# A DLRM tower's interaction layers: three low parts by the adding DMA, 14 tiles split, and the remainder taken from the gathered rows

## The chip, the cores and the metric

One core of one Trainium2 chip. The metric is the device time of one execution in microseconds (us); lower is better. The engines are TensorE (PE in the profile), VectorE (DVE), ScalarE (ACT), GpSimd (POOL) and SyncE (SP), which here only issues DMAs.

## The reference, cut to what matters

For each of B = 1024 samples, 32 ids are looked up in 32 tables of 64-wide rows. Two interaction layers follow, each with a ReLU, whose results are summed over the 64 columns; a small dense network ends it.

```
e = stack([tbl_f[ids[:, f]] for f in range(32)], axis=1)          # (1024, 32, 64)
cin(h, h0, W, b) = relu(einsum('bhd,bmd,ohm->bod', h, h0, W) + b)
x1 = cin(e, e, W1, b1)                                            # 128 outputs
x2 = cin(x1[:, :64], e, W2, b2)                                   # 128 outputs
z  = concat([x1[:, 64:], x2], axis=1).sum(-1)
h  = relu(concat([z, dense_ctx], 1) @ W_top1 + b_top1)
h  = relu(h @ W_top2 + b_top2);  y = h @ W_top3
```

## The kernel before, in words

The samples go in 128 chunks of 8; a chunk has N = 8 x 64 = 512 columns. Two chunks are a pair. Every engine runs a loop of 128 steps (`all_steps`), written by hand, one step for each chunk c; the order of the work is that of the lines in each engine's `step`, and semaphores join the engines. Each engine carries out its own list strictly in order, so what stands behind a wait waits too.

**Gathering.** GpSimd gathers the rows of a pair with four indirect DMAs (L271) into `gathered[s]` (128 partitions, partition = table x 4 + a quarter of the pair's samples), after a small copy of the indices (`place_idx`, L266). SP stores them twice to `emb_rows` in HBM (`store_rows`, L354), so that feature f + shift can be read for any f.

**Layer 1** uses the symmetry of the products: the pairs of features are ordered by their distance (shift). Four tiles `near` (shifts 0 to 15, L239) times `h0` (L236) are multiplied by GpSimd into `prod1` (L308), and go through TensorE as four full-precision tiles of 2 matmuls each (`tiles1`, L592). The products of distance 16 are the *remainder*: 16 for a sample, made from `rem_a` and `rem_b` (`load_rem`, L348, two loads of SP from `emb_rows` for a pair), multiplied by GpSimd (L279), cast to a high part twice by ScalarE (L727, L728), with a low part by GpSimd (L295), all in `rem_parts` of 96 partitions, which one matmul a chunk reads (L595). ScalarE adds the bias, takes the ReLU and the sums (L713, `layer1`, 8 activations of 64 columns).

**Layer 2.** SP copies the first 64 rows of `x1` to all partitions (`replicate_x1`, L248, two DMAs), ScalarE copies them to PSUM (`copy_x1rep`, L762), and VectorE multiplies them with `near` into `pnear` (8 tiles) and with `far` into `pfar` (8 tiles), both L514. Of the 16 tiles 13 are *split* (`T_SPLIT`): a high part in `phi`, rounded by ScalarE (L789 for near tiles 2 to 7, L790 for tiles 0 and 1, L801 for 5 far tiles), and a low part `plo` = product - high part, made by VectorE (L519) for tiles 2 to 12. For the first `T_DMA` = 2 tiles the low part is made otherwise: ScalarE writes the negated high part (L788, `minus_ready`) and an adding DMA of GpSimd adds the product (`low_parts`, L285). A split tile costs 3 matmuls (L604, L605, L610), the other 3 tiles (`whole`, L615) cost 2 slow ones each.

**The steps.** In step c, TensorE does the near high parts of chunk c, layer 1 of chunk c + 2, then `whole`, `low` and the far high parts of chunk c. ScalarE does `layer1(c + 1)`, the minus part, the near casts, the copy of `x1rep` for c + 1, the far cast (behind `acc2_ready` of the chunk before) and `layer2(c - 1)`. SP waits for `z1_ready` of c + 2 (that is `layer1(c + 1)`), replicates `x1`, loads `near` of chunk c + 3 (five DMAs, when VectorE has made `pnear` of c), in even steps stores gathered rows, then loads `far` of c + 2, and in even steps last the remainder rows. In step c of before, TensorE's layer 1 waits for `p1_ready` (L308) and `rem_lo_ready` (L295).

Of the kernel before, what the change touches and what calls it, by code (L numbers as in the profile page):

```python
# [6 lines left out]
F = 32  # L7
D = 64
# [27 lines left out]
T_DMA = 2  # L36
T_FAR = T_NEAR + K2
T_SPLIT = T_FAR + 1
# [4 lines left out]
def build_dlrm(nc, a):  # L43
# [7 lines left out]
    with ctx:  # L51
# [15 lines left out]
        idx = [sb(f"idx_{s}", [P, PAIR_GATHERS], i32) for s in range(3)]  # L67
# [63 lines left out]
        idx_ready = sem("idx_ready")  # L131
# [20 lines left out]
        x1p_ready = sem("x1p_ready")  # L152
        rem_in = sem("rem_in")
# [102 lines left out]
        def _(pool):  # L256
# [8 lines left out]
            def place_idx(pair, s):  # L265
                nc.gpsimd.tensor_copy(idx[s][:, :].unsqueeze(2), idx_all[:, :, bass.ds(pair, 1)]).then_inc(idx_ready, 1)  # L266
                pool.wait_ge(idx_ready, pair + 1)
                pool.sem_inc(lookups_begun, 1)

            def gather(g, s):  # L270
                nc.gpsimd.indirect_dma_start(  # L271
                    out=gathered[s][:, g, :], out_offset=None, in_=a["tables"],
                    in_offset=bass.IndirectOffsetOnAxis(ap=idx[s][:, g:g + 1], axis=0)).then_inc(rows_gathered[s], 16)

            def remainder_products(pair):
                pool.wait_ge(rem_in, 32 * pair + 32)

                pool.wait_ge(rem_lo_ready, pair)
                nc.gpsimd.tensor_tensor(rem_prod[:, :], rem_a[:, :], rem_b[:, :], ALU.mult).then_inc(rem_prod_ready, 1)  # L279
# [8 lines left out]
            for pair in range(3):  # L288
                place_idx(pair, pair)
                for g in range(PAIR_GATHERS):  # L290
                    gather(g, pair)

            def remainder_low(pair):
                pool.wait_ge(rem_hi_ready, pair + 1)
                nc.gpsimd.tensor_tensor(rem_parts[2 * REM:3 * REM, :], rem_prod[:, :],  # L295
                                        rem_parts[0:REM, :].bitcast(fp32), ALU.subtract).then_inc(rem_lo_ready, 1)

            def step(c, turn, u, at):
                pair, odd = turn * (U // 2) + u // 2, u % 2
                if at == 0:  # L300
                    pool.wait_ge(rem_prod_ready, 2)
                    remainder_low(1)
                    pool.wait_ge(rem_lo_ready, 2)
# [8 lines left out]
                if odd and within(at, 3):  # L312
                    remainder_products(pair + 2)
                if not odd and begun(at) and within(at, 2):

                    pool.wait_ge(p1_ready, c + 3)
                    remainder_low(pair + 1)
                    pool.wait_ge(rem_lo_ready, pair + 2)
                if within(at, 7 - odd):
                    if not odd:  # L320
# [4 lines left out]
                        place_idx(pair + 3, u // 2)  # L325
                    for g in range(2 * odd, 2 * odd + 2):
                        gather(g, u // 2)

            remainder_products(1)
# [3 lines left out]
        def _(sp):  # L333
# [28 lines left out]
            store_copy(sp, 0, 0, 0)  # L362
            sp.wait_ge(emb_stored, STORES)
            load_h0(sp, 0, 0, 0)
            load_near_tiles(sp, 0, 0, range(0, K1 // 2))
            load_rem(0)
            load_near(sp, N, 1, 1)
            store_rows(1, 1, 1)
            load_far(0, 0)
            sp.wait_ge(emb_stored, 2 * STORES)  # L370
            sp.wait_ge(rem_prod_ready, 1)
            load_rem(2 * N)
            sp.wait_ge(z1_ready, 1)
            replicate_x1(sp, [0])

# [18 lines left out]
            def step(c, turn, u, at):  # L394
# [33 lines left out]
        def _(dve):  # L428
# [10 lines left out]
            dve.wait_ge(idx_ready, 2)  # L439
# [48 lines left out]
            def products1(s, ks):  # L488
# [7 lines left out]
            dve.wait_ge(rem_in, 32)  # L496
            nc.vector.tensor_tensor(rem_prod[:, :], rem_a[:, :], rem_b[:, :], ALU.mult).then_inc(rem_prod_ready, 1)
# [4 lines left out]
            dve.wait_ge(rem_hi_ready, 1)  # L502
            nc.vector.tensor_tensor(rem_parts[2 * REM:3 * REM, :], rem_prod[:, :],
                                    rem_parts[0:REM, :].bitcast(fp32), ALU.subtract).then_inc(rem_lo_ready, 1)
# [16 lines left out]
            def step(c, turn, u, at):  # L521
# [28 lines left out]
        def _(pe):  # L550
# [43 lines left out]
            def remainder1(s):  # L594
# [245 lines left out]
```

## Time and profile before

| what | us |
|---|---|
| median of 3 runs | 2034.03 |
| lowest and highest of them | 2031.25, 2035.14 |
| the profiled execution | 2035.26 |
| its span in the trace | 2033.5 |
| TensorE busy | 1999.9 |
| VectorE busy | 1923.5 |
| ScalarE busy | 1713.6 |
| GpSimd busy | 1647.3 |
| granted TensorE clock, mean | 0.997 |

The profile is of one execution. "Busy" is the union of the times in which an engine had an instruction under way; the rest is waiting. The span runs from the first to the last instruction of the program; the execution's own time is 1.8 us more.

### The profile page before, as it was taken

Reading aid. Unit: us, or ns where it says so; the run is one execution under the profiler, and the core shown is the slowest. Engines: PE = TensorE matmul, PEld = TensorE weight load, DVE = VectorE, ACT = ScalarE, POOL = GpSimd, SP = SyncE. Lnnn points to the kernel's source line nnn. Section 1 sums busy time; section 2 is a strip of 40 time slices with the busy share of each in tenths; the row PEclk is TensorE's granted clock in tenths of the full one; section 3 lists DMA queues with packets and bytes.
Section 4 is the critical chain, followed back from the end, with each engine's and each line's share of the span. In section 5 each row is a group of like instructions: output and inputs, shape, how many; then the busy total and the mean of one; then the engine's idle time right before and its main releaser. Section 6 shows DMA issues by size and latency. Waiting matters only on the chain.

```text
span 2033.5 us, 24093 instructions
## 1 busy us (share of the span) xinstructions
PE 1999.9 (98%) x7038; PEld 1325.8 (65%) x7038; DVE 1923.5 (95%) x546; ACT 1713.6 (84%) x4887; POOL 1647.3 (81%) x708
## 2 busy tenths in 40 slices
PE   5999999999999999999999999999999999999999
PEld 3666666666666666666666666666666666666664
DVE  6999999999999999999999999999999999999991
ACT  4788888888888888888888888888888888888873
POOL 5898887879899998887889998788999988887520
PEclk9999999999999999999999999999999999999999
DMA  7898988988988989989989989989988989989950
GB/s 227 217 268 235 245 246 232 245 248 232 245 249 234 248 244 235 250 241 236 253 237 237 254 237 236 257 232 237 257 233 238 255 231 239 255 230 238 251 131 11
DMA packets 257782, 474.16 MB, mean 233 GB/s; under 512 B 35425, under 2 KB 52321, under 8 KB 257522
## 3 DMA queue, kind: packets, MB, share of 16 engines
q1 hardware_dynamic: 230450, 396.18, 64.5%
q0 software_dynamic: 26624, 75.52, 22.0%
q8 instruction: 56, 0.92, 0.2%
q10 hardware_dynamic: 576, 0.92, 0.1%
q14 instruction: 76, 0.62, 0.1%
HBM read 321.49 MB, written 16.78 MB: 166 GB/s over the span
## 4 chain that ended last, share of the span: by engine, by line
PE 90%; DMA 3%; DVE 2%; ACT 2%; issue 2%; POOL 1%; SPq 0%; DVEq 0%; POOLq 0%; ACTq 0%
PE acc L592 20%; PE acc L604 17%; PE acc L605 17%; PE acc L610 17%; PE acc L615 14%; DMA plo<-pnear 2%; DVE pnear L514 2%; PE acc L595 1%; ACT phi L789 1%; ACT x L713 1%; POOL prod L308 1%; DMA x1rep<-x 1%; PE x1p L686 0%; DMA near<-emb_rows 0%; PE acc L686 0%
## 5 line engine op out<-in xcount | busy, mean ns | idle before, releaser
L271 POOL DMA_INDIRECT gathered<-in_tables,idx x256 | 655.4, 2560 | 101.8 <-POOL idx L266 51.2
L308 POOL TENSOR_TENSOR prod<-near,h 128x2048 f32<-128x2048 f32 x126 | 582.5, 4623 | 128.5 <-PE acc L595 81.1
L604 PE MATMUL acc<-phi,w2lo 128*128 128x512 f32 x1664 | 655.2, 394 | 8.2 <-ACT phi L789 8.0
L605 PE MATMUL acc<-phi,w2hi 128*128 128x512 f32 x1664 | 654.3, 393 | 0.0
L514 DVE TENSOR_TENSOR pnear<-near,x1p 128x4096 f32<-128x4096 f32 x128 | 564.9, 4413 | 6.2 <-ACT x1p L762 3.8
L514 DVE TENSOR_TENSOR pfar<-far,x1p 128x4096 f32<-128x4096 f32 x128 | 564.9, 4413 | 0.7 <-PE acc L615 0.7
L592 PE MATMUL acc<-prod,w1T 128*128 128x512 f32 x1024 | 460.1, 592 | 1.5 <-DVE prod L489 1.5
L610 PE MATMUL acc<-plo,w2hi 128*128 128x512 f32 x1664 | 454.5, 423 | 0.0
L713 ACT ACTIVATE x<-acc,bias 128x64 f32<-128x64 f32 x1024 | 305.8, 324 | 170.6 <-PE acc L595 170.6
L519 DVE TENSOR_TENSOR plo<-pnear,phi 128x3072 fp32r<-128x3072 f32 x128 | 446.2, 3486 | 0.3 <-ACT phi L789 0.3
L519 DVE TENSOR_TENSOR plo<-pfar,phi 128x2560 fp32r<-128x2560 f32 x128 | 361.2, 2822 | 45.1 <-ACT phi L801 45.0
L610 PEld LDWEIGHTS acc<-plo,w2hi 128*128 128x128 f32 x1664 | 313.0, 188 | 120.6 <-issue 61.0
L604 PEld LDWEIGHTS acc<-phi,w2lo 128*128 128x128 f32 x1664 | 314.1, 189 | 82.3 <-ACT phi L789 12.8
L605 PEld LDWEIGHTS acc<-phi,w2hi 128*128 128x128 f32 x1664 | 314.1, 189 | 67.9
L789 ACT CAST phi<-pnear 128x3072 fp32r<-128x3072 f32 x128 | 352.7, 2756 | 0.0
L615 PE MATMUL acc<-pfar,w2T 128*128 128x512 f32 x768 | 350.6, 592 | 0.0
L592 PEld LDWEIGHTS acc<-prod,w1T 128*128 128x128 f32 x1024 | 193.6, 189 | 197.0 <-issue 184.5
L801 ACT CAST phi<-pfar 128x2560 fp32r<-128x2560 f32 x128 | 299.5, 2340 | 0.0
L713 ACT ACTIVATE acc<-acc,bias 128x64 f32<-128x64 f32 x1024 | 293.5, 291 | 4.8 <-PE acc L605 4.8
L615 PEld LDWEIGHTS acc<-pfar,w2T 128*128 128x128 f32 x768 | 145.7, 190 | 159.3 <-issue 153.7
L713 ACT ACTIVATION_READ_ACCUMULATOR x<-acc,bias 128x1 f32 x1024 | 220.9, 216 | 0.0
L713 ACT ACTIVATION_READ_ACCUMULATOR acc<-acc,bias 128x1 f32 x1024 | 218.1, 213 | 0.0
(75 smaller groups left out, 1151.3 us busy)
## 6 DMA issues: line engine op xcount, KB each, us to landing
far<-emb_rows SPq DMA_DIRECT2D x512, 256.0 KB, 4.6
near<-emb_rows SPq DMA_DIRECT2D x510, 256.0 KB
plo<-pnear POOLq DMA_DIRECT2D x128, 512.0 KB
x1rep<-x SPq DMA_DIRECT2D x255, 256.0 KB, 4.3
h<-emb_rows SPq DMA_DIRECT2D x128, 256.0 KB
emb_rows<-gathered SPq DMA_DIRECT2D x127, 128.0 KB
gathered<-in_tables,idx POOLq DMA_INDIRECT x256, 6.6
rem_a<-emb_rows SPq DMA_DIRECT2D x64, 64.0 KB
```

The costliest lines, as they stand in the source:

```text
L271: nc.gpsimd.indirect_dma_start(out=gathered[s][:, g, :], out_offset=None, in_=a["tables"], in_offset=bass.IndirectOffsetOnAxis(ap=idx[s][: ...
L308: nc.gpsimd.tensor_tensor(prod1[:, :, :], near[(u + 2) % 3][:, :, :], h0[odd][:, :].unsqueeze(1).to_broadcast([P, K1, N]), ALU.mult).then_ ...
L514: return nc.vector.tensor_tensor(out, h0part.unsqueeze(1).to_broadcast([P, A2, k, N]), x1p[s][:, :].rearrange("p (a n) -> p a n", a=A2).un ...
L519: return nc.vector.tensor_tensor(plo[:, parts, :], whole, phi[:, parts, :].bitcast(fp32), ALU.subtract)
L592: nc.tensor.matmul(acc1[s][:, :], w1T[:, k, :], prod1[:, k, :], start=(k == 0), stop=False)
L604: nc.tensor.matmul(acc2[s][:, :], w2lo[:, t, :], phi[:, t, :], start=(t == T_DMA), stop=False)
L605: mm = nc.tensor.matmul(acc2[s][:, :], w2hi[:, t, :], phi[:, t, :], start=False, stop=(t == T_SPLIT - 1))
L610: mm = nc.tensor.matmul(acc2[s][:, :], w2hi[:, t, :], plo[:, t, :], start=False, stop=False)
L615: mm = nc.tensor.matmul(acc2[s][:, :], w2T[:, k, :], pfar[:, 1, K2 - T_WHOLE + k, :], start=False, stop=False)
L713: ins = nc.scalar.activation(out[:, cols], acc[:, cols], ACT.Relu, bias=bias[:, :], accum_out=z[:, bass.ds(c * CB + b, 1)])
L789: nc.scalar.copy(phi[:, T_DMA:T_NEAR, :], products[:, T_DMA:T_NEAR, :]).then_inc(hi_near_ready, 1)
L801: nc.scalar.copy(phi[:, T_NEAR:T_SPLIT, :], pfar[:, :, :, :].rearrange("p a k n -> p (a k) n")[:, 0:T_SPLIT - T_NEAR, :]).then_inc(hi_far_ ...
```

## The change

`T_DMA` goes from 2 to 3 and `T_SPLIT` from 13 to 14, so that 2 tiles stay whole. The gathers read their indices from `idx_all` itself, without the copy. The remainder no longer comes from `emb_rows`: its lower features stand in partitions 0 to 63 of `gathered`, its upper ones are moved beside them by one DMA (`move_upper`); product, high part and low part are made in that layout (64 partitions, 256 elements), and three DMAs a pair (`place_remainder`) carry them to their places in `rem_parts`, of which there are two now. TensorE waits for these DMAs (`rem_in`). ScalarE casts the far tiles ahead of the copy of `x1rep`, and the three tiles of the adding DMA after that; TensorE takes these tiles' high parts behind layer 1. The wait of SP for the stores is at the near load of odd steps.

```diff
-T_DMA = 2
+T_DMA = 3
-T_SPLIT = T_FAR + 1
+T_SPLIT = T_FAR + 2
...
+        rem_b = sb("rem_b", [HALF * GS, PAIR_GATHERS, D])
+        rem_prod = sb("rem_prod", [HALF * GS, PAIR_GATHERS * D])
+        rem_hi = sb("rem_hi", [HALF * GS, PAIR_GATHERS * D], fp32r)
+        rem_lo = sb("rem_lo", [HALF * GS, PAIR_GATHERS * D], fp32r)
+        rem_parts = [sb(f"rem_parts_{s}", [3 * REM, N], fp32r) for s in range(2)]
...
@@ GpSimd
+            def gather(g, pair, s):
...
+                    in_offset=bass.IndirectOffsetOnAxis(ap=idx_all[:, g, pair:pair + 1], axis=0)).then_inc(rows_gathered[s], 16)
+            def remainder_products(pair, s):
+                pool.wait_ge(rem_b_in, 16 * pair + 16)
+                if pair:
+                    pool.wait_ge(rem_lo_ready, pair)
+                nc.gpsimd.tensor_tensor(rem_prod[:, :], gathered[s][0:HALF * GS, :, :].rearrange("p g d -> p (g d)"),
+                                        rem_b[:, :, :].rearrange("p g d -> p (g d)"), ALU.mult).then_inc(rem_prod_ready, 1)
+            def remainder_low(pair):
+                pool.wait_ge(rem_hi_ready, pair + 1)
+                nc.gpsimd.tensor_tensor(rem_lo[:, :], rem_prod[:, :], rem_hi[:, :].bitcast(fp32),
+                                        ALU.subtract).then_inc(rem_lo_ready, 1)
             def step(c, turn, u, at):
                 pair, odd = turn * (U // 2) + u // 2, u % 2
+                if not odd and begun(at) and within(at, 2):
+                    remainder_low(pair + 1)
                 if within(at, 2):
...
                 low_parts(c)
                 if odd and within(at, 3):
-                    remainder_products(pair + 2)
-                if not odd and begun(at) and within(at, 2):
-
-                    pool.wait_ge(p1_ready, c + 3)
-                    remainder_low(pair + 1)
-                    pool.wait_ge(rem_lo_ready, pair + 2)
+                    remainder_products(pair + 2, (u // 2 + 2) % 3)
...
@@ SP
+            def move_upper(pair, s):
+                if pair:
+                    sp.wait_ge(rem_prod_ready, pair)
+                sp.dma_start(rem_b[:, :, :], gathered[s][HALF * GS:F * GS, :, :]).then_inc(rem_b_in, 16)
+            def place_remainder(pair):
+                sp.wait_ge(rem_lo_ready, pair + 1)
+                if pair >= 2:
+                    sp.wait_ge(acc1_ready, 2 * pair - 2)
+                for b, part in enumerate((rem_hi, rem_hi, rem_lo)):
+                    home = rem_parts[pair % 2][b * REM:(b + 1) * REM, :].rearrange("r (w n) -> r w n", w=2)
+                    sp.dma_start(home.bitcast(fp32), part[:, :].bitcast(fp32)).then_inc(rem_in, 16)
...
                     sp.wait_ge(pnear_ready, c + 1)
                     sp.wait_ge(p1_ready, c + 2)
+                    if odd:
+                        sp.wait_ge(emb_stored, STORES * (pair + 3))
                     load_near(sp, (c + 3) * N, 1 - odd, u % 3)
+                if not odd and begun(at) and within(at, 2):
+                    place_remainder(pair + 1)
                 if not odd and within(at, 5):
                     store_rows(pair + 2, (u // 2 + 2) % 3, turn + (u // 2 + 2) // 3 + 1)
+                    move_upper(pair + 2, (u // 2 + 2) % 3)
                 if within(at, 2):
                     sp.wait_ge(pfar_ready, c + 1)
                     load_far((c + 2) * N, odd)
-                if not odd and within(at, 5):
-                    sp.wait_ge(emb_stored, STORES * pair + 3 * STORES)
-                    sp.sem_inc(stores_begun, 1)
-                    sp.wait_ge(rem_prod_ready, pair + 2)
-                    load_rem((c + 4) * N)
@@ VectorE, step
                     dve.wait_ge(lo_near_ready, c)
+                    dve.wait_ge(hi_dma_ready, c)
@@ TensorE, step
                 high(odd, range(T_DMA, T_NEAR))
-                pe.wait_ge(hi_dma_ready, c + 1)
-                high(odd, range(0, T_DMA)).then_inc(hi_near_used, 1)
                 if within(at, 2):
                     pe.wait_ge(p1_ready, c + 3)
-                    pe.wait_ge(rem_lo_ready, pair + 2)
+                    pe.wait_ge(rem_in, 48 * (pair + 2))
                     pe.wait_ge(z1_ready, c + 1)
-                    layer1(odd)
+                    layer1(odd, pair + 1)
...
+                pe.wait_ge(hi_dma_ready, c + 1)
+                high(odd, range(0, T_DMA)).then_inc(hi_near_used, 1)
                 pe.wait_ge(pfar_ready, c + 1)
                 whole(odd).then_inc(far_used, 1)
@@ ScalarE, step
-                if not odd and within(at, 2):
-                    remainder_hi(pair + 1)
...
                 nc.scalar.copy(phi[:, T_DMA:T_NEAR, :], products[:, T_DMA:T_NEAR, :]).then_inc(hi_near_ready, 1)
-                nc.scalar.copy(phi[:, 0:T_DMA, :], products[:, 0:T_DMA, :]).then_inc(hi_dma_ready, 1)
+                act.wait_ge(pfar_ready, c + 1)
+                if begun(at):
+                    act.wait_ge(acc2_ready, c)
+                nc.scalar.copy(phi[:, T_NEAR:T_SPLIT, :], ...).then_inc(hi_far_ready, 1)
                 if within(at, 1):
...
                     copy_x1rep(1 - odd)
-                act.wait_ge(pfar_ready, c + 1)
-                if begun(at):
-                    act.wait_ge(acc2_ready, c)
-                nc.scalar.copy(phi[:, T_NEAR:T_SPLIT, :], ...).then_inc(hi_far_ready, 1)
+                nc.scalar.copy(phi[:, 0:T_DMA, :], products[:, 0:T_DMA, :]).then_inc(hi_dma_ready, 1)
+                if odd and within(at, 3):
+                    remainder_hi(pair + 2)
```

## Rows read from the trace of the kernel before

**Rows 1.** The page: busy us of each engine; the software queue's packets, MB, share.

```profile
PE 1999.9 (98%) x7038; PEld 1325.8 (65%) x7038; DVE 1923.5 (95%) x546; ACT 1713.6 (84%) x4887; POOL 1647.3 (81%) x708
...
q0 software_dynamic: 26624, 75.52, 22.0%
```

**Rows 2.** Chain of waits, 1000 to 1034 us: start us, us, what.

```profile
1001.68 2.58 PE acc L615 x6
1004.26 2.99 PE acc L610 x13
1007.24 0.23 PE acc L604
...
1013.20 3.43 PE acc L592 x8
1016.63 0.24 PE acc L595
...
1028.38 3.43 PE acc L592 x8
```

**Rows 3.** Groups by line and shape: busy us, mean ns of one | idle before.

```profile
L519 DVE TENSOR_TENSOR plo<-pnear,phi 128x3072 fp32r<-128x3072 f32 x128 | 446.2, 3486 | 0.3 <-ACT phi L789 0.3
L519 DVE TENSOR_TENSOR plo<-pfar,phi 128x2560 fp32r<-128x2560 f32 x128 | 361.2, 2822 | 45.1 <-ACT phi L801 45.0
L789 ACT CAST phi<-pnear 128x3072 fp32r<-128x3072 f32 x128 | 352.7, 2756 | 0.0
...
L801 ACT CAST phi<-pfar 128x2560 fp32r<-128x2560 f32 x128 | 299.5, 2340 | 0.0
L713 ACT ACTIVATE acc<-acc,bias 128x64 f32<-128x64 f32 x1024 | 293.5, 291 | 4.8 <-PE acc L605 4.8
...
L790 ACT CAST phi<-pnear 128x1024 fp32r<-128x1024 f32 x128 | 133.9, 1046 | 0.0
L762 ACT COPY x1p<-x1rep 128x1024 f32<-128x1024 f32 x128 | 129.3, 1010 | 11.4 <-DMA x1rep<-x 11.2
...
L728 ACT CAST rem_parts<-rem_prod 32x512 fp32r<-32x512 f32 x64 | 39.7, 620 | 0.8
```

**Rows 4.** Timeline, 1000 to 1034 us: start us, us, instruction [idle before <-releaser].

```profile
1006.97 4.61 SPq L242 DMA_DIRECT2D near<-emb_rows  x4
...
1015.88 4.41 DVE L514 TENSOR_TENSOR pnear<-near,x1p 128x4096 f32<-128x4096 f32 x1
...
1016.90 0.31 ACT L713 ACTIVATE x<-acc,bias 128x64 f32<-128x64 f32 x1 [1.47 <-PE acc L595]
...
1018.35 4.64 POOL L308 TENSOR_TENSOR prod<-near,h 128x2048 f32<-128x2048 f32 x1 [1.55 <-DMA near<-emb_rows]
...
1019.47 1.20 SPq L251 DMA_DIRECT2D x1rep<-x  x2
...
1022.00 4.45 SPq L242 DMA_DIRECT2D near<-emb_rows  x4
```

**Rows 5.** Timeline of the start, 28 to 57 us.

```profile
28.83 0.59 SPq L352 DMA_DIRECT2D rem_b<-emb_rows  x1
...
32.98 1.26 POOL L279 TENSOR_TENSOR rem_prod<-rem_a,rem_b 32x512 f32<-32x512 f32 x1 [6.17 <-DMA rem_b<-emb_rows]
...
48.16 0.99 POOL L285 DMA_DIRECT2D plo<-pnear  x1
...
56.49 4.42 DVE L514 TENSOR_TENSOR pnear<-near,x1p 128x4096 f32<-128x4096 f32 x1 [2.32 <-DMA plo<-pnear]
```

**Rows 6.** Stretches: busy of PE, PEld, DVE, ACT, POOL, then PEclk, DMA share, GB/s.

```profile
62.40:64.70 2.30, 0.01 (x1) 0.00 (x0) 2.30 (x1) 2.30 (x2) 2.10 (x2) 1.00 0.90 269
65.40:68.80 3.40, 3.40 (x10) 2.62 (x9) 3.11 (x1) 3.40 (x4) 3.10 (x2) 0.50 1.06 234
...
1980.20:1984.40 4.20, 0.09 (x1) 0.00 (x0) 4.20 (x2) 3.68 (x3) 0.85 (x1) 0.92 0.17 33
1984.50:1990.50 6.00, 6.00 (x14) 4.74 (x15) 6.00 (x3) 3.10 (x2) 0.00 (x0) 0.50 0.32 59
```

More of the change, by code:

```diff
@@ L288, in _ @@
             for pair in range(3):
-                place_idx(pair, pair)
                 for g in range(PAIR_GATHERS):
-                    gather(g, pair)
+                    gather(g, pair, pair)
+                pool.sem_inc(lookups_begun, 1)
             def remainder_low(pair):
                 pool.wait_ge(rem_hi_ready, pair + 1)
-                nc.gpsimd.tensor_tensor(rem_parts[2 * REM:3 * REM, :], rem_prod[:, :],
-                                        rem_parts[0:REM, :].bitcast(fp32), ALU.subtract).then_inc(rem_lo_ready, 1)
+                nc.gpsimd.tensor_tensor(rem_lo[:, :], rem_prod[:, :], rem_hi[:, :].bitcast(fp32),
+                                        ALU.subtract).then_inc(rem_lo_ready, 1)
             def step(c, turn, u, at):
                 pair, odd = turn * (U // 2) + u // 2, u % 2
[L300 to L303, printed above, removed]
+                if not odd and begun(at) and within(at, 2):
+                    remainder_low(pair + 1)
                 if within(at, 2):
@@ L324, in step @@
                         pool.wait_ge(emb_stored, STORES * pair + STORES)
-                        place_idx(pair + 3, u // 2)
+                        pool.wait_ge(rem_prod_ready, pair + 1)
                     for g in range(2 * odd, 2 * odd + 2):
-                        gather(g, u // 2)
-            remainder_products(1)
+                        gather(g, pair + 3, u // 2)
+            for pair in range(2):
+                remainder_products(pair, pair)
+                remainder_low(pair)
             all_steps(step)
@@ L362, in _ @@
             store_copy(sp, 0, 0, 0)
+            move_upper(0, 0)
             sp.wait_ge(emb_stored, STORES)
@@ L365, in _ @@
             load_near_tiles(sp, 0, 0, range(0, K1 // 2))
-            load_rem(0)
             load_near(sp, N, 1, 1)
             store_rows(1, 1, 1)
+            move_upper(1, 1)
+            place_remainder(0)
             load_far(0, 0)
             sp.wait_ge(emb_stored, 2 * STORES)
-            sp.wait_ge(rem_prod_ready, 1)
-            load_rem(2 * N)
             sp.wait_ge(z1_ready, 1)
             replicate_x1(sp, [0])
+            place_remainder(1)
             sp.wait_ge(tp_copied, 2)
@@ L592, in tiles1, with remainder1, layer1 @@
                     nc.tensor.matmul(acc1[s][:, :], w1T[:, k, :], prod1[:, k, :], start=(k == 0), stop=False)
-            def remainder1(s):
-                nc.tensor.matmul(acc1[s][:, :], w1remT[:, s, :], rem_parts[:, :],
+            def remainder1(s, pair):
+                nc.tensor.matmul(acc1[s][:, :], w1remT[:, s, :], rem_parts[pair % 2][:, :],
                                  start=False, stop=True).then_inc(acc1_ready, 1)
-            def layer1(s):
+            def layer1(s, pair):
                 tiles1(s, range(K1))
-                remainder1(s)
+                remainder1(s, pair)
             def high(s, parts):
@@ L622, in _ @@
             tiles1(0, range(K1 // 2, K1))
-            pe.wait_ge(rem_lo_ready, 1)
-            remainder1(0)
+            pe.wait_ge(rem_in, 48)
+            remainder1(0, 0)
             turn(6, *NEAR_TURNS[1])
@@ L627, in _ @@
             pe.wait_ge(p1_ready, 2)
-            layer1(1)
+            layer1(1, 0)
             pe.wait_ge(x1p_ready, 1)
@@ L726, in remainder_hi @@
                 act.wait_ge(rem_prod_ready, pair + 1)
-                nc.scalar.copy(rem_parts[0:REM, :], rem_prod[:, :])
-                nc.scalar.copy(rem_parts[REM:2 * REM, :], rem_prod[:, :]).then_inc(rem_hi_ready, 1)
+                if pair:
+                    act.wait_ge(rem_in, 48 * pair)
+                nc.scalar.copy(rem_hi[:, :], rem_prod[:, :]).then_inc(rem_hi_ready, 1)
             act.wait_ge(ident_ready, 1)
```

33 lines of the change are left out of this document (5 added, 28 removed).

## The prediction, made before the changed kernel was run

> **What bounds the kernel now.** I read the page first, then the chain of waits in one stretch of the middle, the groups by line and shape, the timeline of the same stretch, and last the start, where the queues are empty. The page [rows 1] shows TensorE busy for 1999.9 of 2033.5 us and VectorE for 1923.5. In the chain from 1000 to 1034 us [rows 2] there is nothing but matmuls end to end: 6 of `whole` in 2.58 us (0.43 each), 13 of `low` in 2.99 (0.23 each), one of `high` every 0.23, 8 of layer 1 in 3.43 and the remainder in 0.24. A chunk is 26 `high`, 13 `low`, 6 `whole`, 8 layer-1 and 1 remainder matmul: 39 x 0.23 + 14 x 0.43 + 0.24 = 15.2 us, and layer 1 starts at 1013.20 and again at 1028.38, 15.18 later. So TensorE sets the pace, 30.4 us for a pair of chunks. VectorE is next to it: 4.4 + 4.4 + 3.5 + 2.8 us = 15.1 [rows 3, 4]. The span is 2033.5 us, the profiled execution 2035.3, 1.3 above the median of 2034.0. About 0.2% (4 us) can be told from no change.
>
> **The change, part by part.**
> *14 tiles split.* `whole` loses 2 matmuls of 0.43, `high` and `low` gain 3 of 0.23: 0.69 - 0.86 = -0.17 us a chunk, x128 = -22 us [rows 2].
> *Three tiles by the adding DMA.* VectorE subtracts 5 near and 6 far tiles in place of 6 and 5, the same elements: 0. ScalarE: L788 and L790 go from 2 tiles to 3; by 1.05 us for 1024 elements and 2.34 for 2560 [rows 3] 1536 take 1.5, so +0.45 each; the near cast falls from 2.76 to 2.34, the far cast rises from 2.34 to 2.76. The software queue takes 22.0% of 16 engines, 447 us in all, 3.5 us a chunk [rows 1]; half as many bytes again bound the extra at 0 and 1.75 us of every DMA engine; I take 1.4, since gathers are a part of that queue.
> *Indices direct.* GpSimd loses 64 small copies and a wait in each. It is not on the path now: 0.
> *Remainder.* GpSimd's two operations shrink from 512 to 256 elements a partition, ScalarE has one cast of at most 0.62 us [rows 3] in place of two (I take 0.35, by half the elements). SP issues for a pair one load of `rem_b` and three placements instead of two loads; at 0.59 us an issue [rows 5] that is +1.2 us. **The place of it is what matters.** `place_remainder(pair + 1)` stands in SP's even step c *behind* `load_near(c + 3)`, and TensorE's `layer1` of the *same* step c now waits for it (`rem_in` of 48 x (pair + 2)). Before, only GpSimd's subtraction stood there.
> *`high(0..2)` behind layer 1.* Layer 1 is reached after 10 `high` matmuls, not 16: 1.4 us sooner. That helps GpSimd's product, and worsens any wait in front of layer 1.
> *Far cast ahead of the copy of `x1rep`.* It takes `acc2_ready` (the end of TensorE's chunk before) ahead of the copy, the dma cast, `layer2` and the next `layer1` on ScalarE, so all of them now start behind that end. Now VectorE waits only a little for the far cast; up to 0.35 us a chunk could be won, but TensorE would cover it.
>
> **When the placement lands.** Take the even step whose near product starts on VectorE at 1015.88 [rows 4]. SP starts to issue `x1rep` at R = 1019.47, and the four near loads from 1022.00 for 4.45 us, until R + 7.0. Three placements of 0.6 bring it to R + 8.8. The lower bound of landing: in the start, with few transfers under way, a remainder load ended its issue at 29.42 and GpSimd used it at 32.98, 3.6 later [rows 5]: R + 12.4. The upper: near loads whose issue ended at 1011.58 let GpSimd go at 1018.35, 6.8 later [rows 4]; the placements, in the same queue behind them, come at R + 7.0 + 6.8, plus up to 1.75 for the adding DMA, which is under way just then, plus 0.2: R + 15.7. I take R + 14.1, between them, nearer the crowded row. The same queue's order is on my side by the Trainium skill too (DMA: Bandwidth & Descriptors, section "Queues, rings and completion order"): on each DMA engine the descriptors are consumed in ring order. By the ~2 us fixed cost of that page (section "Anatomy of one DMA") alone it would be R + 10.8, an estimate, and 100 us less in the end.
>
> If nothing else moved, TensorE would want layer 1 at 4.4 (near product) + 1.5 (minus) + 2.3 (near cast) + 2.3 (10 `high`) behind 1015.88 = 1026.4, and get it at 1019.5 + 14.1 = 1033.6: **7 us idle in each even step**. It cannot be absorbed, since the loop closes. Call W the start of layer 1 in an even step.
> - W to the end of the chunk: layer 1 3.67, 6 `high` 1.37, 4 `whole` 1.72, 14 `low` 3.22, 12 `high` 2.75 = 12.7 [rows 2].
> - ScalarE from there, in its order: far cast 2.76, copy 1.01, dma cast 1.5, remainder cast 0.35, `layer2` 2.4 (8 x 0.29), `layer1` 2.4 (from 1016.90 to about 1019.4) = 10.4; with hand-offs 10.6 [rows 3, 4]. That is the next R. VectorE's branch is as long: far cast 2.76, subtraction of 6 tiles 3.5, near product 4.4 = 10.7.
> - R to the landing 14.1.
>
> Sum: 12.7 + 10.6 + 14.1 = 37.4 us for a pair against 30.4, TensorE idle for 37.4 - 30.0 = 7.4 of them.
>
> *The clock.* What TensorE does after such an idle time has rows: it stood still from 62.41 to 64.70, and the granted clock was 0.50 from 65.4 to 68.8; at the end it stood 4.2 us and ran at 0.50 from 1984.5 to 1990.5 [rows 6]. 3.4 and 6.0 us at 1.2 instead of 2.4 GHz lose 1.7 and 3.0; bounds 0 and 3.0. It falls on the W part of the loop, which is on the path. I take 2.1: 39.5 us a pair. The Trainium skill (TensorE: Matmul & The Clock Gate, section "HAM oscillation — how this bites in real kernels") tells of just this, a kernel that waits for a DMA in every tile and starts each one at half clock; without its effect here the forecast would be 2475.
>
> Even steps with the wait are c = 2 to 124, 62 of them: 62 x (39.5 - 30.4) = +564; start and end nearly as before: **2035 + 564 = about 2600, I say 2595 us**, 28% slower.
>
> **Rivals.**
> *A smaller stall.* Same mechanism, placements at R + 12.4 or sooner, no fall of the clock: 35.7 us a pair, 62 x 5.3 = +329, 2365 us; with near issues as quick as in an empty queue 2 us less again, 2240. For it: the longer period leaves DMA idle. Against: R is followed by near and adding transfers whatever the period. Chance 0.14.
> *TensorE stays the bound, faster.* The price would be the -22 us, 2013 us. It needs the placements to be landed by 1026.4, that is within R + 7.0, which is when the last near load has only been issued. For it: everything else fits, VectorE has no more work. It decides at a landing under R + 7.0; against it stand both rows of landing. Chance 0.09.
> *The adding DMA is the limit.* In the start it was issued at 48.16 and VectorE could go on at 56.49, 8.3 later [rows 5]. Half more bytes make it up to 10; minus ready at 5.9 + 10 = 15.9 against 15.1: at most 0.8 a chunk, +100 us, together with -22 some 2075-2110. It would need the remainder to be hidden. Chance 0.07.
> The forecast has the rest, 0.70.
>
> **Numbers.** Highest case: R + 15.7 and 3.0 of clock, 42.0 a pair, 62 x 11.6: 2755. The likeliest case alone spans 2400 to 2755. For 8 in 10 I go down into the first rival: 2260 to 2740. Faster 0.09 (second rival), within 0.2% 0.03 (out of the third), slower 0.88.
>
> **What would show it.** TensorE idle 6 to 8 us ahead of layer 1 (L592) in every second chunk, released by a DMA into `rem_parts`, 62 times, 400 us or more in all, and none in odd steps; TensorE's busy share near 80%; granted clock below 1 all through the middle; layer-1 starts alternating between about 17 and 22 us apart. On ScalarE the far cast starts right behind TensorE's last `high`. VectorE waits before the far subtraction. Wrong it would be if layer 1 is released by GpSimd's product or by nothing, or if the placements land before the near loads issued ahead of them.

## The result, and the profile after

The changed kernel takes 2690.5 us (median of 4 runs, 2689.2 to 2694.4) against 2034.3: a ratio of 1.323, interval [1.321, 1.326]. The prediction was 2595 us, in a range of 2260 to 2740, with slower at 0.88. The direction and the mechanism came as forecast; the size was 96 us short of 656. In two of the kernels below some executions ran at a lower granted clock and took longer, and the ratios leave them out: two of the four with the placements behind the copies (2460.3 and 2472.8 us), and one of the six with the cast order alone (2556.3 us at a clock of 0.754).

The page of the changed kernel, from its busy times, its clock, its queues and its chain:

```profile
PE 2118.1 (79%) x7166; PEld 1392.4 (52%) x7166; DVE 1930.7 (72%) x544; ACT 1772.4 (66%) x4823; POOL 1390.9 (52%) x646
...
PEclk9988988988889889889889888898898898898889
...
q1 hardware_dynamic: 244786, 404.58, 50.5%
q0 software_dynamic: 26624, 109.08, 22.6%
...
PE 75%; issue 21%; DVE 1%; DMA 1%; ACT 1%; SPq 0%; POOL 0%; DVEq 0%; POOLq 0%; ACTq 0%
PE acc L593 21%; PE acc L605 15%; PE acc L606 15%; PE acc L611 15%; PE acc L616 8%; PE acc L596 1%; DMA plo<-pnear 1%; DVE pnear L514 1%; ACT plo L790 0%; ACT phi L791 0%; PE x1p L687 0%; PE acc L687 0%; ACT phi L795 0%; DMA near<-emb_rows 0%; DVE plo L519 0%
```

TensorE, 98% busy before [rows 1], is at 79%; its clock, 0.997 on average before, drops below full speed in most slices (0.881 on average). The software queue carries 109 MB instead of 75.5. In the chain "issue" grows from 2% to 21%: time in which TensorE waited for something that this view does not name.

The timeline shows where it stands. From an even step to the next (start us, us, instruction, and the idle time before it):

```profile
1287.85 5.58 PE L593 MATMUL acc<-prod,w1T 128*128 128x512 f32 x8 [8.68 <-issue]
...
1292.87 0.80 PE L596 MATMUL acc<-rem_parts,w1remT 96*128 96x512 f32 x1
...
1302.80 2.77 ACT L795 CAST phi<-pfar 128x3072 fp32r<-128x3072 f32 x1 [1.51 <-PE acc L606]
...
1304.84 3.59 PE L593 MATMUL acc<-prod,w1T 128*128 128x512 f32 x8
...
1307.87 0.80 PE L596 MATMUL acc<-rem_parts,w1remT 96*128 96x512 f32 x1
...
1312.98 1.20 SPq L253 DMA_DIRECT2D x1rep<-x  x2
...
1315.42 0.99 POOL L284 DMA_DIRECT2D plo<-pnear  x1 [0.57 <-ACT plo L790]
1315.48 5.42 SPq L244 DMA_DIRECT2D near<-emb_rows  x4
...
1321.00 2.37 SPq L356 DMA_DIRECT2D rem_parts<-rem_hi  x2
...
1323.40 0.60 SPq L356 DMA_DIRECT2D rem_parts<-rem_lo  x1
...
1328.63 2.04 PE L593 MATMUL acc<-prod,w1T 128*128 128x512 f32 x2 [8.62 <-issue]
```

Layer 1 (L593) of the even step starts at 1287.85 after 8.68 us of nothing, of the next even step at 1328.63 after 8.62, and between them lies the odd step's at 1304.84, with no idle time. The remainder's matmuls (L596) stand at 1292.87 and 1307.87, 15.00 apart: that is what one chunk costs where there is no wait, against 15.2 before. The pair takes 40.8. The placements are issued at 1321.00 and 1323.40, behind the near loads (1315.48, 5.42 us), and TensorE goes on 4.6 us after the last was issued. What ends the wait is in the trace too: in each of the 62 even steps layer 1 starts 0.09 us after the landing of that step's last placement. The waits, in total, with their number and the longest:

```profile
PE acc L593 <- issue: 534.4, 62, 9.5
DVE pfar L514 <- PE acc L616: 533.1, 62, 9.2
...
ACT x L714 <- PE acc L596: 583.2, 64, 9.8
...
DVE pnear L514 <- DMA plo<-pnear: 57.0, 69, 3.8
```

62 times TensorE stands, 534 us in all, and each of the 62 is handed on: VectorE's far product waits 533 us for `whole`, ScalarE's `layer1` 583 us for layer 1. All the waits are one wait, seen from each engine. Busy times in stretches around it (us, busy of PE, PEld, DVE, ACT, POOL, then PEclk, DMA share, GB/s):

```profile
1279.30:1287.80 8.50, 0.00 (x0) 0.00 (x0) 7.82 (x3) 5.12 (x19) 1.05 (x1) 0.63 0.99 268
1287.90:1292.00 4.10, 4.10 (x6) 1.79 (x7) 0.05 (x1) 0.00 (x0) 0.00 (x0) 0.54 0.48 174
1292.00:1304.80 12.80, 12.80 (x51) 9.39 (x50) 7.25 (x2) 8.20 (x19) 9.57 (x4) 1.00 0.56 124
```

In the idle stretch the DMA engines are at 0.99 of their time: they are moving `x1`, the near rows, the adding DMA and last the placements. In the 4 us behind it the granted clock is 0.54, and layer 1 takes 5.58 us in place of 3.59.

### The profile page after: what moved, and what is told of

Same layout as the page of the kernel before. It is cut to its first block, busy times and chain, and to the rows that moved or that the text cites. A ratio compares the mean times of both kernels' runs of the same rounds, so it can differ in the third digit from the quotient of the medians.

```text
span 2689.9 us, 24288 instructions
## 1 busy us (share of the span) xinstructions
PE 2118.1 (79%) x7166; PEld 1392.4 (52%) x7166; DVE 1930.7 (72%) x544; ACT 1772.4 (66%) x4823; POOL 1390.9 (52%) x646
## 3 DMA queue, kind: packets, MB, share of 16 engines
q0 software_dynamic: 26624, 109.08, 22.6%
## 4 chain that ended last, share of the span: by engine, by line
PE 75%; issue 21%; DVE 1%; DMA 1%; ACT 1%; SPq 0%; POOL 0%; DVEq 0%; POOLq 0%; ACTq 0%
PE acc L593 21%; PE acc L605 15%; PE acc L606 15%; PE acc L611 15%; PE acc L616 8%; PE acc L596 1%; DMA plo<-pnear 1%; DVE pnear L514 1%; ACT plo L790 0%; ACT phi L791 0%; PE x1p L687 0%; PE acc L687 0%; ACT phi L795 0%; DMA near<-emb_rows 0%; DVE plo L519 0%
## 5 line engine op out<-in xcount | busy, mean ns | idle before, releaser
L593 PE MATMUL acc<-prod,w1T 128*128 128x512 f32 x1024 | 591.4, 731 | 536.3 <-issue 534.4
L605 PE MATMUL acc<-phi,w2lo 128*128 128x512 f32 x1792 | 704.3, 393 | 4.9 <-ACT phi L803 3.0
L606 PE MATMUL acc<-phi,w2hi 128*128 128x512 f32 x1792 | 703.1, 392 | 0.0
L593 PEld LDWEIGHTS acc<-prod,w1T 128*128 128x128 f32 x1024 | 237.6, 240 | 829.8 <-issue 822.0
L268 POOL DMA_INDIRECT gathered<-in_tables,idx_all x256 | 552.4, 2158 | 72.0 <-issue 68.4
L519 DVE TENSOR_TENSOR plo<-pfar,phi 128x3072 fp32r<-128x3072 f32 x128 | 429.8, 3358 | 103.6 <-ACT phi L795 102.7
L795 ACT CAST phi<-pfar 128x3072 fp32r<-128x3072 f32 x128 | 354.6, 2771 | 143.5 <-PE acc L606 138.4
L519 DVE TENSOR_TENSOR plo<-pnear,phi 128x2560 fp32r<-128x2560 f32 x128 | 366.3, 2862 | 0.3
L791 ACT CAST phi<-pnear 128x2560 fp32r<-128x2560 f32 x128 | 297.7, 2326 | 0.0
L790 ACT ACTIVATE plo<-pnear 128x1536 fp32r<-128x1536 f32 x128 | 191.0, 1492 | 134.0 <-PE acc L611 86.9
L616 PE MATMUL acc<-pfar,w2T 128*128 128x512 f32 x512 | 240.5, 592 | 0.0
```

Of the source, the lines that this page charges most:

```text
L268: nc.gpsimd.indirect_dma_start(out=gathered[s][:, g, :], out_offset=None, in_=a["tables"], in_offset=bass.IndirectOffsetOnAxis(ap=idx_all[ ...
L519: return nc.vector.tensor_tensor(plo[:, parts, :], whole, phi[:, parts, :].bitcast(fp32), ALU.subtract)
L593: nc.tensor.matmul(acc1[s][:, :], w1T[:, k, :], prod1[:, k, :], start=(k == 0), stop=False)
L605: nc.tensor.matmul(acc2[s][:, :], w2lo[:, t, :], phi[:, t, :], start=(t == T_DMA), stop=False)
L606: mm = nc.tensor.matmul(acc2[s][:, :], w2hi[:, t, :], phi[:, t, :], start=False, stop=(t == T_SPLIT - 1))
L616: mm = nc.tensor.matmul(acc2[s][:, :], w2T[:, k, :], pfar[:, 1, K2 - T_WHOLE + k, :], start=False, stop=False)
```

## The experiments

R is the start of the first copy of `x1` in SP's even step, W the start of layer 1 in TensorE's same step. "Of the trace" below means an average over 53 even steps of the middle (61 in what concerns landings and near loads), from the start times of the instructions and the landings that the trace gives.

**Placements behind the copies of x1, ahead of the near loads.**

```diff
                     replicate_x1(sp, range(A2))
+                if not odd and begun(at) and within(at, 2):
+                    place_remainder(pair + 1)
                 if within(at, 3):
...
                     load_near(sp, (c + 3) * N, 1 - odd, u % 3)
-                if not odd and begun(at) and within(at, 2):
-                    place_remainder(pair + 1)
```

> The changed kernel, but in SP's even step the three placements of the remainder are issued behind the two copies of x1 and ahead of the near loads. Theory (TensorE waits for placements that stand behind the near loads): they are issued by R + 3.1 and land at R + 7 to 8, which is about when TensorE reaches layer 1; the near loads come 1.8 us later. The pair falls from 41 us to 30.2 - 32, the time to 2020 - 2130 us. Rival (the longer adding DMA, or the cast order on ScalarE, is what costs): stays above 2500 us.

Measured: 2422.3 and 2433.3 us, ratio 1.193 [1.190, 1.196]; the trace is of an execution of 2460.3 us. Neither theory's number. The timeline of an even step:

```profile
1320.66 1.20 SPq L253 DMA_DIRECT2D x1rep<-x  x2
...
1321.96 3.05 SPq L356 DMA_DIRECT2D rem_parts<-rem_hi  x2
...
1323.11 0.99 POOL L284 DMA_DIRECT2D plo<-pnear  x1 [0.73 <-ACT plo L790]
...
1325.06 1.51 SPq L356 DMA_DIRECT2D rem_parts<-rem_lo  x1
...
1331.93 2.04 PE L593 MATMUL acc<-prod,w1T 128*128 128x512 f32 x2 [4.21 <-issue]
```

The first two placements take 3.05 us to issue and the third 1.51; in between, at R + 2.5, GpSimd issues the adding DMA. Layer 1 starts at R + 11.3, not R + 7 to 8: the placements now stand ahead of the near loads, but the adding DMA, in another queue, is issued among them. Of the trace, the first placement, issued 1.3 us ahead of the adding DMA, lands 4.5 us after its issue began, the other two 7.0; the last lands at R + 11.2, the adding DMA at R + 10.8 and the near loads at R + 16.0. The stall shrinks from 8.6 to 4.2 us, and the loop, 11.3 + 26.0 from W back to R of the trace = 37.3 us a pair, gives 2034 + 62 x 6.9, about 2460 us, the time of that execution. So the place of the placements is a cause, and a place ahead in its own queue's list does not alone make a DMA early. That the adding DMA is what delays them here fits these landings; no run takes it out at this place.

**Placements at the top of the even step.**

```diff
             def step(c, turn, u, at):
                 pair, odd = turn * (U // 2) + u // 2, u % 2
+                if not odd and begun(at) and within(at, 2):
+                    place_remainder(pair + 1)
                 if within(at, 1):
                     sp.wait_ge(z1_ready, c + 2)
...
-                if not odd and begun(at) and within(at, 2):
-                    place_remainder(pair + 1)
```

> The changed kernel, but the three placements are issued at the top of SP's even step, ahead of the wait for z1_ready. There SP waits anyway; the low part is ready some 3 us before R, so they land at about R + 2, well before TensorE wants them. Theory: no wait for the remainder is left, and the time is 2013 us if TensorE is the bound (15.02 us a chunk), or 2075 to 2110 us if the adding DMA of 768 KB, 9 us from issue to landing in the changed kernel's trace, holds back VectorE's next near product. Rival (SP now waits for the low part and delays the copies of x1): 2150 us or more, with waits of SP on GpSimd.

Measured: 2124.7 us, ratio 1.042 [1.040, 1.045]. Moving one call takes 566 of the 656 us away. TensorE no longer waits ahead of layer 1; the median placement lands 3.4 us after its issue began, against 5.3 in the changed kernel. What is left is 15 us above the range for a late adding DMA. Groups by line and shape (busy us, mean ns | idle before, releaser):

```profile
L306 POOL TENSOR_TENSOR prod<-near,h 128x2048 f32<-128x2048 f32 x126 | 585.6, 4647 | 418.9 <-DMA near<-emb_rows 410.4 <-PE acc L596 8.1
L514 DVE TENSOR_TENSOR pnear<-near,x1p 128x4096 f32<-128x4096 f32 x128 | 565.9, 4421 | 119.7 <-DMA plo<-pnear 115.2 <-ACT x1p L766 3.8
```

VectorE's near product waits 115 us for the adding DMA, and GpSimd's product 410 us for near loads.

**Fillers ahead of the wait.**

```diff
-                    pe.wait_ge(rem_in, 48 * (pair + 2))
                     pe.wait_ge(z1_ready, c + 1)
+                    if not odd and begun(at):
+                        for _ in range(8):
+                            nc.tensor.matmul(acc1[0][:, :], w1T[:, 0, :], flat(w1T[:, 0:N // O, :]), start=True, stop=True)
+                    pe.wait_ge(rem_in, 48 * (pair + 2))
                     layer1(odd, pair + 1)
```

> The changed kernel, with 8 full-precision matmuls of no use (16 of 0.43 us, 6.9 us in all) into acc1[0] in each even step, ahead of TensorE's wait for the remainder. They fit in the idle 8.6 us. Theory (the fall of the clock behind the idle time is on the path): the granted clock stays at 1.0 and the time falls by 62 x (1.7 to 2.1) = 105 to 130 us, to 2560 - 2585 us. Rival (the clock's loss is hidden, the loop is closed by others): 2685 - 2695 us with the clock at 1.0.

Measured: 2577.6 us (2 runs, 2574.2 and 2581.1), the clock 0.994 and 0.992. That is 113 us or 1.8 us a pair less, for 496 full-precision matmuls more. Of the trace, W to the far cast falls from 15.07 to 13.30 us, and the two other parts of the loop stay within 0.05. And with the engine busy up to the wait, the group of layer 1 now names its releaser:

```profile
L593 PE MATMUL acc<-prod,w1T 128*128 128x512 f32 x1024 | 478.1, 611 | 109.0 <-DMA rem_parts<-rem_lo 107.5 <-DVE prod L494 1.5
```

The DMA into `rem_parts` it is. The mean matmul falls from 731 to 611 ns, near the 592 of before.

**The wait behind the tiles of layer 1.**

```diff
-                    pe.wait_ge(rem_in, 48 * (pair + 2))
                     pe.wait_ge(z1_ready, c + 1)
-                    layer1(odd, pair + 1)
+                    tiles1(odd, range(K1))
+                    pe.wait_ge(rem_in, 48 * (pair + 2))
+                    remainder1(odd, pair + 1)
```

> The changed kernel, with the wait for the remainder moved behind the eight tile matmuls of layer 1: only the remainder's own matmul waits. Theory (the loop is landing, TensorE to the chunk's end, ScalarE to R, landing): the TensorE part shrinks by 3.4 us, so 62 x 3.4 = -211 us, some 2480 us; a little less still (2450) if less of the rest falls on the low clock. Rival (the period is set by DMA transfers alone): 2690 us.

Measured: 2478.3 us. The loop's arithmetic holds: 3.43 us of matmuls taken out of the part behind the landing took 3.46 us off a pair (40.95 to 37.49 of the trace). The wait, in the waits of this kernel:

```profile
PE acc L596 <- DMA rem_parts<-rem_lo: 311.3, 62, 6.0
```

**The late placements with the amounts of before.**

```diff
-T_DMA = 3
+T_DMA = 2
-T_SPLIT = T_FAR + 2
+T_SPLIT = T_FAR + 1
```

> The changed kernel with its late placements, but T_DMA = 2 and T_SPLIT = 13. It asks how much of the 15.7 us from R (the first copy of x1) to layer 1 in an even step comes from the adding DMA's third tile. Theory (the third tile stands between, about 1.5 us of every DMA engine): 14.2 us from R to layer 1, the rest of the loop as before (0.17 us more for whole tiles, 0.4 less in the dma cast and 0.4 less in the far cast), so some 2.2 us less a pair, 2540 - 2570 us. Rival (the landing is set by SP's issues and the near loads alone): 15.7 us again, 0.7 less a pair, about 2645 us.

Measured: 2482.0 us, ratio 1.220 [1.218, 1.222]: 58 us under the expected range, and far from the rival. The timeline:

```profile
1323.18 1.20 SPq L253 DMA_DIRECT2D x1rep<-x  x2
...
1325.67 5.82 SPq L244 DMA_DIRECT2D near<-emb_rows  x4
...
1332.90 0.60 SPq L356 DMA_DIRECT2D rem_parts<-rem_lo  x1
...
1336.70 1.76 PE L593 MATMUL acc<-prod,w1T 128*128 128x512 f32 x2 [5.00 <-issue]
```

From R to W it is 13.5 us here and 13.66 of the trace, 15.73 in the changed kernel: the third tile, the only difference in what the DMAs carry, is worth 2.07 us. ScalarE's part from the far cast to R fell by 0.83 as expected; but from W to the far cast it fell by 0.50 (15.07 to 14.57), where I had added 0.17 for the slow tiles. I wrote 2.2 us a pair together; it was 3.4. The 0.17 was wrong for this part: with T_DMA = 2 two `high` matmuls more stand ahead of layer 1, so behind it there are 4 `high` and 1 `low` fewer and 2 `whole` more, -5 x 0.23 + 2 x 0.43 = -0.29. The rest is the clock: from W to the remainder's matmul an even step takes 4.89 us here and 5.12 in the changed kernel, 0.23 less, at a granted clock of 0.63 against 0.60. Why the clock was a little higher, no run shows.

The two parts of the change do not simply add. Of the 656 us the amounts take 208 with the late placements (2690.5 to 2482.0) and 90 with the early ones (2124.7 to 2034.8, in the next experiment); the late place costs 566 us with the new amounts and 447 with the old.

**The amounts, with the placements first.** The kernel with the placements at the top, at T_DMA = 2 and T_SPLIT = 13 (as before), and at T_DMA = 2 and T_SPLIT = 14:

> Placements first in SP's even step, and T_DMA = 2 and T_SPLIT = 13 as before the change: the remainder from the gathered rows, the direct indices and the cast order alone. Theory (what is left of the loss, 2125 against 2034 us, comes from the third tile of the adding DMA): TensorE is the bound again at 15.19 us a chunk, 2028 to 2040 us. Rival (the four small DMAs of the remainder, or the far cast ahead of the copy, cost it): 2070 us or more.

> Placements first, T_DMA = 2 and T_SPLIT = 14: the 14th split tile without the third tile of the adding DMA, so VectorE subtracts 12 tiles and not 11. By its rows VectorE then needs 4.4 + 4.4 + 3.4 + 3.4 = 15.6 us a chunk less some 0.3 of overlap: 15.3 to 15.6, against 15.02 of TensorE. Theory (VectorE is the bound): 2050 to 2090 us, less than with the third DMA tile (2125). Rival (the DMA tile is not what costs): 2125 us or more.

Measured: 2034.8 us, ratio 1.000 [0.999, 1.001]; and 2037.0, ratio 1.001 [1.000, 1.002]. So the remainder from the gathered rows, the direct indices and the order of the casts cost nothing once the placements are early, and win nothing. The 14th split tile costs 2 us instead of the 2050 to 2090 us expected: VectorE's four instructions take 4.41 + 4.41 + 3.38 + 3.35 = 15.55 by their means, and of the trace its period is 15.21, so the overlaps are 0.34, a little more than the 0.3 that I had allowed. The third DMA tile alone, from this kernel to the one with the placements first, costs 88 us. The same groups as above:

```profile
L306 POOL TENSOR_TENSOR prod<-near,h 128x2048 f32<-128x2048 f32 x126 | 582.5, 4623 | 252.4 <-DMA near<-emb_rows 246.8 <-PE acc L596 4.2 <-issue 0.6
L514 DVE TENSOR_TENSOR pnear<-near,x1p 128x4096 f32<-128x4096 f32 x128 | 564.7, 4412 | 7.0 <-ACT x1p L766 3.8 <-DMA plo<-pnear 3.1
```

The wait of the near product for the adding DMA goes from 3.1 to 115.2 us, that of GpSimd for near loads from 247 to 410.

In the kernel with the old amounts that second wait is 303 us, at 2034.8 us in all, so it need not cost anything.

**The amounts in the kernel before.** T_DMA = 3 and T_SPLIT = 14, nothing else:

> The kernel before, with T_DMA = 3 and T_SPLIT = 14 only. Theory (the adding DMA of 768 KB lands about 9 us behind its issue and holds back VectorE's near product): 15.7 us a chunk and more, 2085 to 2150 us, with VectorE waiting for the adding DMA. Rival (TensorE stays the bound and gains 0.17 us a chunk): 2010 to 2016 us.

Measured: 2192.3 us, ratio 1.078 [1.076, 1.080]. Slower, as the theory had it, but above its range and for another reason. VectorE waits 202 us for the far cast (L801), and the period is 16.5 us on average:

```profile
1308.74 4.42 DVE L514 TENSOR_TENSOR pnear<-near,x1p 128x4096 f32<-128x4096 f32 x1
...
1313.19 1.49 ACT L788 ACTIVATE plo<-pnear 128x1536 fp32r<-128x1536 f32 x1 [2.56 <-DVE pnear L514]
...
1314.58 2.31 ACT L789 CAST phi<-pnear 128x2560 fp32r<-128x2560 f32 x1
...
1316.80 1.47 ACT L790 CAST phi<-pnear 128x1536 fp32r<-128x1536 f32 x1
...
1318.18 1.00 ACT L762 COPY x1p<-x1rep 128x1024 f32<-128x1024 f32 x1
...
1319.12 2.76 ACT L801 CAST phi<-pfar 128x3072 fp32r<-128x3072 f32 x1
...
1321.91 3.36 DVE L519 TENSOR_TENSOR plo<-pfar,phi 128x3072 fp32r<-128x3072 f32 x1 [0.66 <-ACT phi L801]
```

Near product 4.42, minus part 1.49, near cast 2.31, dma cast 1.47, copy 1.00, far cast 2.76, far subtraction 3.36: 16.8, less the overlaps 16.5. ScalarE's five operations in a row have grown by 0.8 us and VectorE's far subtraction by 0.5, and all of them stand between two near products. In the kernel before the same sum, with its own durations [rows 3, 4] and the minus part of this line,

```profile
1005.21 1.06 ACT L788 ACTIVATE plo<-pnear 128x1024 fp32r<-128x1024 f32 x1 [1.02 <-DVE pnear L514]
```

is 4.41 + 1.06 + 2.76 + 1.05 + 1.01 + 2.34 + 2.82 = 15.45, less the overlaps just under TensorE's 15.2: it was a hair from being the bound.

**The cast order.** In the kernel before, alone, and with the amounts:

```diff
+                act.wait_ge(pfar_ready, c + 1)
+                if begun(at):
+                    act.wait_ge(acc2_ready, c)
+                nc.scalar.copy(phi[:, T_NEAR:T_SPLIT, :], ...).then_inc(hi_far_ready, 1)
                 if within(at, 1):
                     act.wait_ge(x1rep_in, 16 * A2 * c + 32 * A2)
...
                     copy_x1rep(1 - odd)
-                act.wait_ge(pfar_ready, c + 1)
-                if begun(at):
-                    act.wait_ge(acc2_ready, c)
-                nc.scalar.copy(phi[:, T_NEAR:T_SPLIT, :], ...).then_inc(hi_far_ready, 1)
```

> The kernel before, with ScalarE's far cast moved ahead of the copy of x1rep only. Theory (the wait for the end of TensorE's chunk then stands ahead of the copy and of layer2, but is short while TensorE is not held up): 2030 to 2040 us, no change; VectorE's wait of 45 us for the far cast gets shorter. Rival (the copy comes too late for VectorE's next near product, or ScalarE's chain gets too long): over 2045 us.

> The kernel before with T_DMA = 3, T_SPLIT = 14 and the far cast ahead of the copy of x1rep. With the amounts alone the period was 16.45 us, and that is a loop of VectorE and ScalarE: near product 4.42, minus part 1.49, near cast 2.31, dma cast 1.48, copy 1.0, far cast 2.76, far subtraction 3.36, less 0.4 of overlaps. Theory (that loop): without the copy in it 15.45 us a chunk, 128 x 1.0 less than 2192, that is 2065 us; or up to 2125 if the adding DMA and the near loads bound it as in the kernel with the placements first. Rival (the adding DMA alone made the 16.45): 2180 us or more.

Alone: 2028.1 us, ratio 0.997 [0.995, 0.998], 6 us faster than the kernel before, below the expected 2030 to 2040. With the amounts: 2121.6 us, ratio 1.042 [1.041, 1.044]: it repays 71 of the 158 us, so the loop of VectorE and ScalarE was that part, and the total is that of the placements first (2124.7), which has the same amounts. The waits in it are others, though:

```profile
L308 POOL TENSOR_TENSOR prod<-near,h 128x2048 f32<-128x2048 f32 x126 | 588.0, 4667 | 70.3 <-DMA near<-emb_rows 69.7
L514 DVE TENSOR_TENSOR pnear<-near,x1p 128x4096 f32<-128x4096 f32 x128 | 565.6, 4418 | 49.2 <-DMA plo<-pnear 44.1 <-ACT x1p L762 3.9
```

VectorE stands 44 us for the adding DMA and, by its own group, 69 us for the far cast; there it was 115 and 6. And GpSimd waits 70 us for near loads, not 410, in the same total: those 410 are not what costs the time. VectorE's subtractions in the cast-order kernel:

```profile
L519 DVE TENSOR_TENSOR plo<-pnear,phi 128x3072 fp32r<-128x3072 f32 x128 | 466.8, 3647 | 12.0 <-ACT phi L789 11.5
...
L519 DVE TENSOR_TENSOR plo<-pfar,phi 128x2560 fp32r<-128x2560 f32 x128 | 360.0, 2812 | 0.0
```

The 45 us of waiting for the far cast [rows 3] are gone. The near subtraction got longer (3486 to 3647 ns), which ate part of it. TensorE's period is 15.19 averaged over the middle, where it was 15.22 before: that is 4 of the 6 us.

**Two variants that were to gain more.** The cast order with T_SPLIT = 14, and with the gathers reading `idx_all` directly (in GpSimd and without VectorE's wait for the copies):

> The kernel before with T_SPLIT = 14 (T_DMA stays 2) and the far cast ahead of the copy: TensorE 15.02 us a chunk, VectorE 4.33 + 4.33 + 3.3 + 3.3 = 15.2. Theory (VectorE is the bound at 15.2, TensorE's saving is not to be had): 2028 to 2040 us, no better than with the cast order alone (2028). Rival (TensorE is the bound): 2006 us.

> The kernel before with the far cast ahead of the copy, and the gathers reading idx_all itself (no copies of the indices, and VectorE does not wait for them in the start). Theory (GpSimd is off the path in the loop, but the first gather comes 1 us and VectorE's first weights up to 6 us sooner in the start): 2022 to 2028 us, 0 to 6 us below the cast order alone. Rival (VectorE and GpSimd get in each other's way in the start): 2028 to 2035 us.

Measured: 2037.8 us, ratio 1.002 [1.001, 1.002], and 2031.3 us, ratio 0.998 [0.997, 0.999]. The first as expected: VectorE, idle for 7 us in its four groups, takes the bound at 15.27 and the 0.17 us a chunk of TensorE is not to be had. The second is 3 us above the cast order alone, outside its expectation; direct indices gain nothing.

The changes together, in this order of adding them: cast order -6, amounts with it +93 (2028.1 to 2121.6), remainder and indices about 0 (2121.6 against 2124.7), the place of three DMAs +566: 2690.

## Why the prediction was right, and the term that was too small

**The wait.** That TensorE would stand 6 to 8 us ahead of layer 1 in every second chunk, 62 times, behind a DMA into `rem_parts`: it was 62 times, 8.6 us, and the last placement's landing stands 0.09 us ahead of each start of layer 1. The page alone did not show it: it wrote "issue", that is nothing, which was on my list of signs of being wrong. The other signs came: TensorE busy for 79%, no wait in odd steps, layer-1 starts 17.1 and 23.8 us apart by turns (forecast 17 and 22). Placed early, the same DMAs cost none of the 566 us. The adding DMA has a part in the wait too: with its third tile a late placement comes 2.07 us later.

**The loop of 39.5 us a pair.** It was 40.95: over 62 pairs 90 of the missing 96 us. Its parts, as predicted and of the trace:

| part | predicted | measured |
|---|---|---|
| W to the start of the far cast | 12.7 + 2.1 of clock | 15.07 |
| far cast to R | 10.6 | 10.16 |
| R to W | 14.1 | 15.73 |

The clock's 2.1 fits: from W to the remainder's matmul an even step takes 5.1 us and an odd one 3.03, and the fillers gave back 1.8 of it. The term that was too small is R to W, "between them, nearer the crowded row": of the 1.45 us that the sum lacks it makes +1.6, W to the far cast +0.3 and the far cast to R -0.4. It lay on its upper bound of 15.7. Three things were under-sized in it. I took the near loads' issue from one row, 4.45 us, and that row was a low one: over 61 even steps of the kernel before it is 5.54 on average, as in the very next one,

```profile
1052.38 5.75 SPq L242 DMA_DIRECT2D near<-emb_rows  x4
```

and 5.45 in the changed kernel. I took a placement at 0.6 us from the start, where fewer transfers were under way; the first two took 2.2 together. So the last was issued at R + 10.3 on average, not R + 8.2. And the third tile of the adding DMA was worth 2.07 us, not 1.4. The crowded row itself was right: in the kernel with the fillers, whose trace has these landings, the near loads land 6.9 us after the end of their issue (the row had 6.8), at R + 14.9, and the last placement 0.7 later.

The Trainium skill's ~2 us of fixed cost (DMA: Bandwidth & Descriptors, section "Anatomy of one DMA"), which the page gives for DMAs that GpSimd issues, would behind that last issue give an estimate of R + 12.9, 2.8 us short: the landing is set by what else is in the queues. (The prediction puts its own R + 10.8 at 100 us less; by its loop it is 62 x 3.3 = 205.) The order within SP's queue, which I had from the same page, agrees with both traces: placements issued behind the near loads land behind them, those issued ahead land ahead, at R + 11.2 against 16.0. But it gives no time, since placements ahead of the near loads still took 11.3 us.

**Costs of single operations.** These fit. Groups of the changed kernel:

```profile
L519 DVE TENSOR_TENSOR plo<-pfar,phi 128x3072 fp32r<-128x3072 f32 x128 | 429.8, 3358 | 103.6 <-ACT phi L795 102.7
L519 DVE TENSOR_TENSOR plo<-pnear,phi 128x2560 fp32r<-128x2560 f32 x128 | 366.3, 2862 | 0.3
L795 ACT CAST phi<-pfar 128x3072 fp32r<-128x3072 f32 x128 | 354.6, 2771 | 143.5 <-PE acc L606 138.4 <-DVE pfar L514 3.7 <-issue 1.4
...
L791 ACT CAST phi<-pnear 128x2560 fp32r<-128x2560 f32 x128 | 297.7, 2326 | 0.0
...
L790 ACT ACTIVATE plo<-pnear 128x1536 fp32r<-128x1536 f32 x128 | 191.0, 1492 | 134.0 <-PE acc L611 86.9 <-DVE pnear L514 47.1
L803 ACT CAST phi<-pnear 128x1536 fp32r<-128x1536 f32 x128 | 188.1, 1469 | 0.0
...
L731 ACT CAST rem_hi<-rem_prod 64x256 fp32r<-64x256 f32 x64 | 25.7, 402 | 17.2 <-issue 14.7 <-POOL rem_prod L277 2.5
```

The minus part and the dma cast are 1.49 and 1.47 (predicted 1.5), the near cast 2.33 (2.34), the far cast 2.77 (2.76), the remainder cast 0.40 (0.35). VectorE's two subtractions are 6.2 us together against 6.3.

**The rivals.** TensorE as the bound at 2013 us never came, not even with the placements early, because the third rival then holds. That one had 2075 to 2110 us; it is 2122 to 2125. I put its whole effect in VectorE's wait, at most 0.8 us a chunk; with the placements first that wait is 115 us, 0.9 a chunk. How the rest comes about stays open; GpSimd's longer waits for near loads are not it, by the cast-order kernel with the same amounts. And the far cast order, costed at nothing, is worth 71 us under these amounts: without it the third rival would have been 2192. I had seen ScalarE's chain only with the new order. The prediction counts casts as beside other work; the sum from one near product to the next, 15.45 against 15.2, would have shown how little cover there was.

## What to carry to other kernels

When a wait is moved from an engine's result to a DMA that carries it, find the place of that DMA in its queue's list and add up everything that is issued ahead of it and beside it in the same step; then close the loop from the waiting engine back to that issue, since a late transfer is paid once in every round of it. Issue a small transfer that somebody waits for where its queue stands idle anyway, not behind large loads. And when a tile is handed to a DMA, ask which transfers share the engines at that moment: the tile costs them its time too.

## What was not expected of the hardware

- A DMA issued ahead of 1.25 MB of loads in its own queue still landed 6.9 us after its issue began, with a 768 KB adding DMA of another queue issued among the three placements; issued at the top of the step, the median placement landed in 3.4.
- 256 KB more in the adding DMA made the placements land 2.07 us later. In the changed kernel the software queue's share of the engines is 22.6% of a 32% longer span for 109 MB, 608 us against 447 for 75.5 MB: 33.5 MB cost 161 us of all 16 engines, 1.25 us a chunk; that leaves 0.8 of the 2.07 us for waiting around it, by this estimate.
- The granted clock is 0.63 on average already within the idle 8.5 us and 0.54 in the 4.1 us after it, and back to 1.00 by the remainder's matmul: layer 1 of an even step lost 2.1 us so against that of an odd one, and filling the wait with matmuls gave back 1.8 a pair. That agrees with the Trainium skill's account of a kernel that waits for a DMA in every tile and starts each at half clock (TensorE: Matmul & The Clock Gate, section "HAM oscillation — how this bites in real kernels").
